# Fused attention plus mixture layer: score chunks of one key tile grouped before their exp drain

## The chip, the cores and the metric

One Trainium2 chip, all 8 NeuronCores, one launch. Times are device microseconds of the slowest core. The cores don't exchange data: each pair of cores takes one of four sequences. Even cores take query rows 0 to 2559 of it, odd cores rows 2560 to 4095.

## The reference, cut to what matters

The layer is feed-forward (8 experts, top 2), causal attention, feed-forward, each with a layer norm ahead and a residual. The change lies in the attention:

```python
q = jnp.concatenate([q_C.reshape(B, T, H, HS), q_R], axis=-1)
k = jnp.concatenate([k_C.reshape(B, T, H, HS), broadcast(k_R)], axis=-1)
att = jnp.einsum('bqhd,bkhd->bhqk', q, k) / jnp.sqrt(HS + DHR)
att = jnp.where(jnp.tril(jnp.ones((T, T), bool)), att, -jnp.inf)
att = softmax(att)
y = jnp.einsum('bhqk,bkhd->bqhd', att, v.reshape(B, T, H, HS)).reshape(B, T, C)
return y @ W_O
```

B = 4, T = 4096, C = 1024, H = 16, HS = 64, DHR = 32. Matmuls run in bf16 with fp32 accumulation.

## The kernel before, in words

Each engine (t PE, v DVE, s ACT, g POOL, y SP) gets a list of instructions that is written out by hand in the order of the Python code; an engine runs its list in order. `em.op` adds an instruction, `em.w` a wait on a semaphore, `em.drain` an instruction that ends when the engine's work ahead of it has ended and then signals. `Rot` hands out buffer slots in turn: `acquire` adds the waits that were left by whoever last released the slot.

The stages follow each other with a barrier between: layer norm, gate, feed-forward (first product at L381, second at L470), layer norm, keys and values, compressed queries (L698), then four quarters of four heads, each with a query stage (L756 and L759), a value stage and `attn_quarter`, and then the output projection, layer norm, gate and feed-forward. Even cores have 20 key tiles and 20 query tiles of 128 rows; odd cores have 32 key tiles and 12 query tiles (first query tile q0 = 20).

`attn_quarter` goes through its four heads. For each it builds the head's keys (L897), and then walks sections of up to 8 query tiles: an odd core has one section of 8 tiles and one of 4, an even core 8, 8 and 4. For each key tile of a section up to the last one its queries may see, the live queries are cut into chunks of up to 512. For one chunk PE writes scores to an accumulator slot (L927; three slots, PA0, PA1 and PM, rotation `pa_rot`), ACT takes the exponential into SBUF (L935; four buffers, `pt_rot`) and drains, on a key tile on the diagonal DVE multiplies the first 128 queries by the mask (L943), and PE multiplies by the values and adds into the section's accumulator `pav` of two banks (L960). Where a chunk crosses a bank, L960 is issued in two pieces. In PE's list the value matmul of a chunk stands right behind the wait for ACT's drain, and the next chunk's score matmul behind it. After a section, DVE takes a row of `pav`, SP moves it by a DMA, DVE takes the reciprocal (L980), PE spreads it over 64 rows (L992) and DVE scales (L996).

Of the kernel before, what the change touches and what calls it, by code (L numbers as in the profile page):

```python
# [864 lines left out]
def attn_quarter(em, d, s, p, nkt, ntt, q0, hq):  # L865
    S = em.sem
    pbig = p["big"]
    nk = nkt * 128

    secs = []  # L870
    t0 = 0
    while t0 < ntt:
        secs.append((t0, min(t0 + 8, ntt)))
        t0 += 8

    kh_rot = Rot(2, em)
    pa_rot = Rot(3)
    pt_rot = Rot(4)
    yev_rot = Rot(2, em)
    kc_rot = Rot(2)  # L880
    lsem = em.dsem()
    for hl in range(4):
        h = hq * 4 + hl
        ksl = kh_rot.acquire(em, "v")
        kh = s["khat"][:, ksl * T: ksl * T + T]
        em.op("v", lambda v, kh=kh: v.memset(kh[64:128, 0:nk], 0.0))
        em.drain("v", inc=S["DV"])
        dv_z = S["DV"].v
        em.w("y", S["DV"], dv_z)
        em.dma("y", kh[64:96, 0:nk], s["kr"][:, 0:nk], kh_rot.sems[ksl])  # L890
        em.dma("y", kh[96:97, 0:nk], d["onesr"][0:1, 0:nk], kh_rot.sems[ksl])
        la_kr = kh_rot.sems[ksl].v
        for tc in range(nk // 512):
            csl = kc_rot.acquire(em, "t")
            pk = pbig[0:64, PB1 + csl * 512: PB1 + csl * 512 + 512]
            for cc in range(2):
                em.op("t", lambda t, pk=pk, cc=cc, h=h, tc=tc: t.matmul(  # L897
                    pk, s["wukb"][:, cc * C + h * 64: cc * C + h * 64 + 64],
                    s["ckv"][:, cc * T + tc * 512: cc * T + tc * 512 + 512],
                    start=(cc == 0), stop=(cc == 1), skip_group_check=True),  # L900
                    inc=(S["PE"] if cc == 1 else None))
            pe_kc = S["PE"].v
            em.w("v", S["PE"], pe_kc)
            em.op("v", lambda v, kh=kh, pk=pk, tc=tc: v.tensor_copy(
                kh[0:64, tc * 512: tc * 512 + 512], pk), inc=S["DV"])
            kc_rot.release((S["DV"], S["DV"].v))
        em.drain("v", inc=S["DV"])
        dv_kh = S["DV"].v
        em.w("t", kh_rot.sems[ksl], la_kr)
        em.w("t", S["DV"], dv_kh)  # L910

        for (st_, en) in secs:
            seclen = (en - st_) * 128
            pav = pbig[0:65, PB0: PB0 + seclen]
            kmax = q0 + en
            first_kt = True
            for kt in range(kmax):
                qlo = max(st_, kt - q0)
                cols0 = qlo * 128
                ncols = (en - qlo) * 128  # L920
                diag = (kt - q0 == qlo and kt >= q0 + st_)
                for ch in range((ncols + 511) // 512):
                    cw = min(512, ncols - ch * 512)
                    co = cols0 + ch * 512
                    psl = pa_rot.acquire(em, "t")
                    ps = pbig[:, (PA0, PA1, PM)[psl]: (PA0, PA1, PM)[psl] + cw]
                    em.op("t", lambda t, ps=ps, kh=kh, kt=kt, hl=hl, co=co, cw=cw: t.matmul(  # L927
                        ps, kh[:, kt * 128:(kt + 1) * 128],
                        s["qh"][:, hl * NTMAX + co: hl * NTMAX + co + cw],
                        start=True, stop=True), inc=S["PE"])  # L930
                    pe_s = S["PE"].v
                    tsl = pt_rot.acquire(em, "s")
                    ptb = s["pt"][:, tsl * 512: tsl * 512 + cw]
                    em.w("s", S["PE"], pe_s)
                    em.op("s", lambda sc, ptb=ptb, ps=ps: sc.activation(  # L935
                        ptb, ps, AF.Exp), inc=S["AC"])
                    em.drain("s", inc=S["AC"])
                    ac_e = S["AC"].v
                    pa_rot.release((S["AC"], ac_e))
                    dv_m = None  # L940
                    if diag and ch == 0:
                        em.w("v", S["AC"], ac_e)
                        em.op("v", lambda v, ptb=ptb: v.tensor_mul(  # L943
                            ptb[:, 0:128], ptb[:, 0:128], s["dmask"][:, :]))
                        em.drain("v", inc=S["DV"])
                        dv_m = S["DV"].v
                    em.w("t", S["AC"], ac_e)
                    if dv_m is not None:
                        em.w("t", S["DV"], dv_m)
                    off0 = co - st_ * 128  # L950
                    pieces = []
                    o_, rel_ = off0, 0
                    while rel_ < cw:
                        w_ = min(cw - rel_, 512 - (o_ % 512))
                        pieces.append((o_, rel_, w_))
                        o_ += w_
                        rel_ += w_
                    for pi, (po, pr, pw) in enumerate(pieces):
                        em.op("t", lambda t, pav=pav, ptb=ptb, kt=kt, hl=hl,
                              po=po, pr=pr, pw=pw, fk=first_kt: t.matmul(  # L960
                            pav[:, po: po + pw],
                            s["vhat"][:, kt * 260 + hl * 65: kt * 260 + (hl + 1) * 65],
                            ptb[:, pr: pr + pw],
                            start=fk, stop=False, skip_group_check=True),
                            inc=(S["PE"] if pi == len(pieces) - 1 else None))
                    pt_rot.release((S["PE"], S["PE"].v))
                first_kt = False
            em.drain("t", inc=S["PE"])
            pe_av = S["PE"].v
            em.w("v", S["PE"], pe_av)  # L970
            em.op("v", lambda v, pav=pav, seclen=seclen: v.tensor_copy(
                s["lr"][64:65, 0:seclen], pav[64:65, 0:seclen]))
            em.drain("v", inc=S["DV"])
            dv_l = S["DV"].v
            em.w("y", S["DV"], dv_l)
            em.w("y", lsem, lsem.v)
            em.dma("y", s["lr"][0:1, 0:seclen], s["lr"][64:65, 0:seclen], lsem)
            la_l = lsem.v
            em.w("v", lsem, la_l)
            em.op("v", lambda v, seclen=seclen: v.reciprocal(  # L980
                s["lr"][0:1, 0:seclen], s["lr"][0:1, 0:seclen]))
            em.drain("v", inc=S["DV"])
            for ch in range((seclen + 511) // 512):
                cw = min(512, seclen - ch * 512)
                esl = yev_rot.acquire(em, "v")
                yb = s["yev"][0:64, esl * 512: esl * 512 + cw]
                em.op("v", lambda v, yb=yb, pav=pav, ch=ch, cw=cw: v.tensor_copy(
                    yb, pav[0:64, ch * 512: ch * 512 + cw]))
                em.drain("v", inc=S["DV"])
                em.w("t", S["DV"], S["DV"].v)  # L990
                prl = pbig[0:64, PM: PM + cw]
                em.op("t", lambda t, prl=prl, ch=ch, cw=cw: t.matmul(  # L992
                    prl, s["ones1f"][0:1, 0:64], s["lr"][0:1, ch * 512: ch * 512 + cw],
                    start=True, stop=True), inc=S["PE"])
                em.w("v", S["PE"], S["PE"].v)
                em.op("v", lambda v, yb=yb, prl=prl: v.tensor_tensor(  # L996
                    yb, yb, prl, ALU.mult))
                em.drain("v", inc=S["DV"])
                dv_y = S["DV"].v
                em.w("y", S["DV"], dv_y)  # L1000
                em.dma("y", d["d_yn"][h, :, q0 * 128 + st_ * 128 + ch * 512:
                                      q0 * 128 + st_ * 128 + ch * 512 + cw], yb,
                       yev_rot.sems[esl])
                yev_rot.release((yev_rot.sems[esl], yev_rot.sems[esl].v))
            em.w("t", S["DV"], S["DV"].v)
        kh_rot.release((S["PE"], S["PE"].v))
    yev_rot.finish(em, "y")
    kh_rot.finish(em, "y")
    em.w("y", lsem, lsem.v)
# [461 lines left out]
```

How the kernel before makes its waits and increments, by code:

```python
    def w(self, e, sem, val=None):  # L54
        if self.stopped:
            return
        v = sem.v if val is None else val
        if v <= 0:
            return
        self.q[e].append(lambda eng, s=sem.h, v=v: eng.wait_ge(s, v))
# [1 line left out]
    def op(self, e, fn, inc=None, n=1):  # L62
        if self.stopped:
            return None
        if inc is None:
            self.q[e].append(lambda eng, fn=fn: fn(eng))
            return None
        inc.v += n
        self.q[e].append(lambda eng, fn=fn, s=inc.h, n=n: fn(eng).then_inc(s, n))
        return inc.v
# [1 line left out]
    def drain(self, e, inc=None, n=1):  # L72
        if self.stopped:
            return None
        if inc is None:
            self.q[e].append(lambda eng: eng.drain())
            return None
        inc.v += n
        self.q[e].append(lambda eng, s=inc.h, n=n: eng.drain().then_inc(s, n))
        return inc.v
# [1 line left out]
    def dma(self, e, dst, src, sem):  # L82
        if self.stopped:
            return None
        sem.v += 16
        self.q[e].append(
            lambda eng, dst=dst, src=src, s=sem.h: eng.dma_start(dst, src).then_inc(s, 16))
        return sem.v
```

## Time and profile before

| | |
|---|---|
| median of 3 runs | 9474.25 us (9413.29 to 9484.06) |
| the profiled execution | 9392.34 us |
| its span, slowest core (7) | 9390.8 us |
| PE, DVE, ACT busy on that core | 5106.9, 1689.4, 1432.2 us |

The spans of odd cores are 9363 to 9391 us, those of even cores 9019 to 9031 us. The profile shows one core (the slowest, unless another is named). In the rows below a group or a timeline entry names line, engine, operation, output and input; "x" is a count; a number in square brackets is idle time of the engine just before, and what ended it. L79 is the helper that writes drains: "ACTq L79" is a drain on ACT's queue. "pbig" is the accumulator memory.

### The profile page before, as it was taken

How to read it: one execution, taken by the hardware profiler on the slowest of the kernel's cores; microseconds unless marked ns; L12 is line 12 of the kernel's file. 1: busy time of each engine (PE TensorE's matmuls, PEld its weight loads, DVE VectorE, ACT ScalarE, POOL GpSimd, SP SyncE). 2: the span in 40 equal slices, each digit the busy share in tenths (PEclk: the TensorE clock that was granted, in tenths of full speed). 3: DMA queues.
4: the chain of work that ended last, by engine and by line, in shares of the span. 5: the costliest groups of instructions: out<-in, count | busy, mean ns of one | idle time of the engine just before them, and what ended most of it. 6: DMA issues, size and time to landing. Idle time of an engine off the chain costs nothing.

```text
span 9390.8 us, 65490 instructions; the slowest of 8 cores (9019.2 to 9390.8 us)
## 1 busy us (share of the span) xinstructions
PE 5106.9 (54%) x18300; PEld 1838.5 (20%) x18300; DVE 1689.4 (18%) x3215; ACT 1432.2 (15%) x2340; POOL 302.3 (3%) x576
## 2 busy tenths in 40 slices
PE   1389996665565335534444444444444444359655
PEld 0234442222222112201101111101111111123222
DVE  4233330000000321121112111121112111223100
ACT  1033330000000100012220222022211222113000
POOL 0000000000000000100010000100010000010000
PEclk9999997777788668855556555655556555679877
DMA  4465543224333433300012000300011000466343
GB/s 163 115 160 156 158 149 63 61 61 96 98 92 101 159 110 91 91 7 3 2 15 60 2 2 3 71 2 2 4 27 46 2 2 3 139 156 165 74 103 94
DMA packets 874165, 683.01 MB, mean 73 GB/s; under 512 B 489584, under 2 KB 791664, under 8 KB 873152
## 3 DMA queue, kind: packets, MB, share of 16 engines
q1 hardware_dynamic: 792224, 584.56, 21.9%
q0 software_dynamic: 81584, 94.16, 6.1%
q8 instruction: 167, 2.74, 0.1%
q14 instruction: 190, 1.56, 0.1%
HBM read 582.45 MB, written 180.36 MB: 81 GB/s over the span
## 4 chain that ended last, share of the span: by engine, by line
PE 46%; DMA 16%; DVE 9%; ACT 9%; SPq 6%; issue 6%; DVEq 2%; POOL 2%; PEldq 1%; ACTq 1%; PEld 0%; POOLq 0%
PE pbig L470 15%; PE pbig L381 12%; PE pbig L960 8%; ACT sb_pt L935 8%; SPq L87 6%; PE pbig L927 6%; DMA sb_hld<-d_h 5%; DMA sb_xnld<-d_xnA 2%; DVEq L79 2%; DMA sb_cqld<-d_cq 2%; DMA d_cq<-sb_cqst 2%; DVE sb_lr L980 2%; PE pbig L756 1%; DMA sb_xt<-d_x 1%; PE pbig L992 1%
## 5 line engine op out<-in xcount | busy, mean ns | idle before, releaser
L470 PE MATMUL pbig<-sb_w2b,sb_hld 128*128 128x512 bf16 x5632 | 1402.9, 414 | 978.0 <-DMA sb_hld<-d_h 978.0
L960 PE MATMUL pbig<-sb_pt,sb_vhat 128*65 128x512 bf16 (+3 forms) x1392 | 782.1, 569 | 1220.4 <-ACTq L79 1003.2
L381 PE MATMUL pbig<-sb_xnld,sb_w1b 128*128 128x512 bf16 x5632 | 1264.1, 386 | 123.0 <-DMA sb_xnld<-d_xnA 123.0
L935 ACT ACTIVATE sb_pt<-pbig 128x512 bf16<-128x512 f32 (+1 forms) x1344 | 771.8, 574 | 2309.5 <-PE pbig L927 2309.5
L470 PEld LDWEIGHTS pbig<-sb_w2b,sb_hld 128*128 128x128 bf16 x5632 | 581.4, 105 | 1779.3 <-issue 1241.7
L927 PE MATMUL pbig<-sb_qh,sb_khat 128*128 128x512 bf16 (+1 forms) x1344 | 809.1, 602 | 34.8 <-DVEq L79 34.8
L381 PEld LDWEIGHTS pbig<-sb_xnld,sb_w1b 128*128 128x128 bf16 x5632 | 551.9, 99 | 813.4 <-issue 190.0
L393 ACT ACTIVATE sb_hrelu<-pbig,sb_b1c 128x512 bf16<-128x512 f32 x704 | 483.9, 687 | 1394.5 <-PE pbig L381 1337.8
L402 DVE TENSOR_TENSOR sb_hst<-sb_hrelu,pbig 128x512 bf16<-128x512 bf16 x704 | 473.9, 686 | 978.6 <-ACT sb_hrelu L393 568.1
L960 PEld LDWEIGHTS pbig<-sb_pt,sb_vhat 128*65 128x65 bf16 x1392 | 179.4, 132 | 2217.8 <-issue 2217.8
L943 DVE TENSOR_TENSOR sb_pt<-sb_pt,sb_dmask 128x128 bf16<-128x128 bf16 x192 | 43.2, 225 | 2495.4 <-ACTq L79 2495.4
L756 PE MATMUL pbig<-sb_cqld,sb_wuqh 128*128 128x512 bf16 x768 | 249.4, 408 | 280.7 <-DMA sb_wqrh<-wqr 161.0
L192 ACT ACTIVATE sb_sqs<-sb_xt 128x1024 bf16<-128x1024 f32 x76 | 80.3, 1056 | 1910.6 <-DMA sb_xt<-d_x 1889.3
L246 PE MATMUL pbf<-sb_cidb,sb_xnt 128*128 128x128 bf16 x608 | 76.9, 306 | 502.1 <-DVEq L79 502.1
L698 PE MATMUL pbig<-sb_xnld,sb_wdqh 128*128 128x512 bf16 x768 | 194.7, 403 | 135.7 <-DVE sb_cqst L706 71.8
L992 PE MATMUL pbig<-sb_lr,sb_ones1f 1*64 1x512 f32 x96 | 92.8, 1068 | 317.8 <-DVEq L79 317.8
L503 DVE TENSOR_TENSOR sb_ypld<-sb_ypld,pbig 128x1024 f32<-128x1024 f32 x44 | 53.7, 1221 | 1172.1 <-PE pbig L480 1122.6
L491 DVE COPY sb_yt<-pbig 128x1024 f32<-128x1024 f32 x44 | 53.9, 1225 | 1069.8 <-PE pbig L470 1069.8
L87 POOL DMA_DIRECT2D sb_wuqh<-wuq x128 | 102.8, 803 | 3187.4 <-SPq L79 3187.4
L811 ACT ACTIVATE sb_q2s<-sb_qh 96x512 bf16<-96x512 bf16 x48 | 30.2, 630 | 1097.3 <-DVEq L79 964.1
L980 DVE RECIPROCAL sb_lr<-sb_lr 1x1024 f32<-1x1024 f32 (+1 forms) x32 | 158.1, 4941 | 61.0 <-DMA sb_lr<-sb_lr 61.0
L246 PEld LDWEIGHTS pbf<-sb_cidb,sb_xnt 128*128 128x128 bf16 x608 | 58.8, 137 | 520.1 <-issue 520.1
(112 smaller groups left out, 2351.5 us busy)
## 6 DMA issues: line engine op xcount, KB each, us to landing
sb_xnld<-d_xnA SPq DMA_DIRECT2D x704, 128.0 KB, 2.9
d_h<-sb_hst SPq DMA_DIRECT2D x704, 128.0 KB, 1.9
sb_hld<-d_h SPq DMA_DIRECT2D x352, 256.0 KB, 4.7
sb_xt<-d_x SPq DMA_DIRECT2D x112, 512.0 KB, 5.0
sb_xt<-x SPq DMA_DIRECT2D x96, 512.0 KB, 5.3
sb_cqld<-d_cq SPq DMA_DIRECT2D x384, 128.0 KB, 2.2
sb_w1b<-w POOLq DMA_DIRECT2D x128, 256.0 KB, 9.1
sb_w2b<-w POOLq DMA_DIRECT2D x128, 256.0 KB, 20.6
```

What stands on the lines that cost most here:

```text
L79: self.q[e].append(lambda eng, s=inc.h, n=n: eng.drain().then_inc(s, n))
L87: lambda eng, dst=dst, src=src, s=sem.h: eng.dma_start(dst, src).then_inc(s, 16))
L381: em.op("t", lambda t, ph=ph, wsl=wsl, xsl=xsl, xc=xc, ht=ht: t.matmul(ph, s["w1b"][:, wsl * 8 * C + xc * C + ht * 128: wsl * 8 * C + xc * ...
L393: em.op("s", lambda sc, rb=rb, ph=ph, e=e, ht=ht: sc.activation(rb, ph, AF.Relu, bias=s["b1c"][:, e * 8 + ht: e * 8 + ht + 1]), inc=S["AC"])
L402: em.op("v", lambda v, ob=ob, rb=rb, pw=pw: v.tensor_tensor(ob, rb, pw, ALU.mult), inc=S["DV"])
L470: half=half, k=k, last=last, pa=pa: t.matmul(ph, s["hld"][:, lsl * 4096 + ei * 1024 + hc * 128: lsl * 4096 + ei * 1024 + hc * 128 + 128], ...
L698: em.op("t", lambda t, ps=ps, xsl=xsl, xc=xc, cq=cq: t.matmul(ps, s["wdqh"][:, xc * 2048 + cq * 128: xc * 2048 + cq * 128 + 128], s["xnld" ...
L756: em.op("t", lambda t, ps=slots[dt], cqc=cqc, dt=dt, cl=cl: t.matmul(ps, s["wuqh"][:, cqc * 256 + dt * 128: cqc * 256 + dt * 128 + 128], c ...
L927: em.op("t", lambda t, ps=ps, kh=kh, kt=kt, hl=hl, co=co, cw=cw: t.matmul(ps, kh[:, kt * 128:(kt + 1) * 128], s["qh"][:, hl * NTMAX + co: ...
L935: em.op("s", lambda sc, ptb=ptb, ps=ps: sc.activation(ptb, ps, AF.Exp), inc=S["AC"])
L960: po=po, pr=pr, pw=pw, fk=first_kt: t.matmul(pav[:, po: po + pw], s["vhat"][:, kt * 260 + hl * 65: kt * 260 + (hl + 1) * 65], ptb[:, pr: p ...
L980: em.op("v", lambda v, seclen=seclen: v.reciprocal(s["lr"][0:1, 0:seclen], s["lr"][0:1, 0:seclen]))
```

## The change

All chunks of a key tile (two where more than 512 queries are live, else one) now form a group. First come the score matmul and the exp of every chunk, each with its own slots, without a drain between the exps; then one drain of ACT, whose value releases all score slots of the group; the mask multiply of a diagonal tile and PE wait for that one value; then come all value matmuls.

```diff
+                chinfo = []
                 for ch in range((ncols + 511) // 512):
...
                     em.op("s", lambda sc, ptb=ptb, ps=ps: sc.activation(
                         ptb, ps, AF.Exp), inc=S["AC"])
-                    em.drain("s", inc=S["AC"])
-                    ac_e = S["AC"].v
-                    pa_rot.release((S["AC"], ac_e))
-                    dv_m = None
-                    if diag and ch == 0:
-                        em.w("v", S["AC"], ac_e)
-                        em.op("v", lambda v, ptb=ptb: v.tensor_mul(
-                            ptb[:, 0:128], ptb[:, 0:128], s["dmask"][:, :]))
-                        em.drain("v", inc=S["DV"])
-                        dv_m = S["DV"].v
-                    em.w("t", S["AC"], ac_e)
-                    if dv_m is not None:
-                        em.w("t", S["DV"], dv_m)
+                    chinfo.append((psl, tsl, ptb, co, cw))
+                em.drain("s", inc=S["AC"])
+                ac_grp = S["AC"].v
+                for psl, _, _, _, _ in chinfo:
+                    pa_rot.release_slot(psl, (S["AC"], ac_grp))
+                dv_m = None
+                if diag:
+                    em.w("v", S["AC"], ac_grp)
+                    em.op("v", lambda v, ptb=chinfo[0][2]: v.tensor_mul(
+                        ptb[:, 0:128], ptb[:, 0:128], s["dmask"][:, :]))
+                    em.drain("v", inc=S["DV"])
+                    dv_m = S["DV"].v
+                em.w("t", S["AC"], ac_grp)
+                if dv_m is not None:
+                    em.w("t", S["DV"], dv_m)
+                for psl, tsl, ptb, co, cw in chinfo:
                     off0 = co - st_ * 128
                     pieces = []
...
-                    pt_rot.release((S["PE"], S["PE"].v))
+                    pt_rot.release_slot(tsl, (S["PE"], S["PE"].v))
```

PE's list on an odd core, first key tiles of the section of 8 query tiles, with each instruction's waits (AC is ACT's semaphore, DV is DVE's, D9 a DMA's), before:

```order
L927 MATMUL pbig<-sb_qh,sb_khat 128x512 [waits D9,DV]
L960 MATMUL pbig<-sb_pt,sb_vhat 65x512 [waits AC]
L927 MATMUL pbig<-sb_qh,sb_khat 128x512
L960 MATMUL pbig<-sb_pt,sb_vhat 65x512 [waits AC]
L927 MATMUL pbig<-sb_qh,sb_khat 128x512
```

and of the changed kernel (scores are L928 there, values L964):

```order
L928 MATMUL pbig<-sb_qh,sb_khat 128x512 [waits D9,DV]
L928 MATMUL pbig<-sb_qh,sb_khat 128x512
L964 MATMUL pbig<-sb_pt,sb_vhat 65x512 [waits AC]
L964 MATMUL pbig<-sb_pt,sb_vhat 65x512
L928 MATMUL pbig<-sb_qh,sb_khat 128x512
```

The second score matmul of a key tile moved ahead of the first value matmul, and one of two waits on ACT before a value matmul is gone.

The same list at key tile 21, with 512 and 384 live queries, on the diagonal, before:

```order
L927 MATMUL pbig<-sb_qh,sb_khat 128x512 [waits AC]
L960 MATMUL pbig<-sb_pt,sb_vhat 65x384 [waits AC,DV]
L960 MATMUL pbig<-sb_pt,sb_vhat 65x128
L927 MATMUL pbig<-sb_qh,sb_khat 128x384 [waits AC]
L960 MATMUL pbig<-sb_pt,sb_vhat 65x384 [waits AC]
L927 MATMUL pbig<-sb_qh,sb_khat 128x512 [waits AC]
```

and of the changed kernel:

```order
L928 MATMUL pbig<-sb_qh,sb_khat 128x512 [waits AC]
L928 MATMUL pbig<-sb_qh,sb_khat 128x384 [waits AC]
L964 MATMUL pbig<-sb_pt,sb_vhat 65x384 [waits AC,DV]
L964 MATMUL pbig<-sb_pt,sb_vhat 65x128
L964 MATMUL pbig<-sb_pt,sb_vhat 65x384
L928 MATMUL pbig<-sb_qh,sb_khat 128x512 [waits AC]
```

The wait for the mask (DV) now stands behind both score matmuls; the pieces of the value matmul are the same. The order of ACT's exps and of DVE's instructions is unchanged.

## Rows read from the trace of the kernel before

**Rows 1.** Spans and granted clock of an even and an odd core
```profile
core 6: 9026.7 us, clock 0.710
...
core 7: 9390.8 us, clock 0.705
```

**Rows 2.** The page's chain that ended last, shares by line
```profile
PE pbig L470 15%; PE pbig L381 12%; PE pbig L960 8%; ACT sb_pt L935 8%; SPq L87 6%; PE pbig L927 6%; DMA sb_hld<-d_h 5%; DMA sb_xnld<-d_xnA 2%; DVEq L79 2%; DMA sb_cqld<-d_cq 2%; DMA d_cq<-sb_cqst 2%; DVE sb_lr L980 2%; PE pbig L756 1%; DMA sb_xt<-d_x 1%; PE pbig L992 1%
```

**Rows 3.** Source line L935 (ns min/median/max, starts), and L927's 512-column group by form
```profile
L935 ACT ACTIVATE sb_pt<-pbig x1344: 277/597/598, 4118.7 to 8023.1; 128x512 bf16<-128x512 f32 x176, 128x384 bf16<-128x384 f32 x16
...
L927 PE MATMUL pbig<-sb_qh,sb_khat 128*128 128x512 bf16 x1200 | 748.7, 624 | 34.8 <-DVEq L79 34.8
```

**Rows 4.** Core 7, timeline in a section of 8 query tiles (start us, us)
```profile
7900.36 0.61 PE L960 MATMUL pbig<-sb_pt,sb_vhat 128*65 128x512 bf16 x1 [0.87 <-ACTq L79]
...
7900.76 0.63 PE L927 MATMUL pbig<-sb_qh,sb_khat 128*128 128x512 bf16 x1
7901.49 0.60 ACT L935 ACTIVATE sb_pt<-pbig 128x512 bf16<-128x512 f32 x1 [1.31 <-PE pbig L927]
...
7902.26 0.61 PE L960 MATMUL pbig<-sb_pt,sb_vhat 128*65 128x512 bf16 x1 [0.87 <-ACTq L79]
...
7913.70 0.61 PE L960 MATMUL pbig<-sb_pt,sb_vhat 128*65 128x512 bf16 x1 [0.87 <-ACTq L79]
```

**Rows 5.** Timeline of PE alone, matmuls back to back in L756
```profile
3893.83 1.01 PE L756 MATMUL pbig<-sb_cqld,sb_wuqh 128*128 128x512 bf16 x2 [42.05 <-DMA sb_wqrh<-wqr]
...
3895.06 1.06 PE L756 MATMUL pbig<-sb_cqld,sb_wuqh 128*128 128x512 bf16 x2
3895.91 0.63 PE L759 MATMUL pbig<-sb_cqld,sb_wqrh 128*128 128x512 bf16 x1
```

**Rows 6.** Timeline: ACT at L192, and the first exp of a quarter
```profile
3176.51 1.06 ACT L192 ACTIVATE sb_sqs<-sb_xt 128x1024 bf16<-128x1024 f32 x1
3177.48 0.18 ACT L192 ACTIVATION_READ_ACCUMULATOR sb_sqs<-sb_xt 128x1 f32 x1
...
4116.97 0.38 PE L927 MATMUL pbig<-sb_qh,sb_khat 128*128 128x512 bf16 x1 [0.98 <-DVEq L79]
4117.43 1.28 ACT L935 ACT_TABLE_LOAD   x1 [51.69 <-PE pbig L927]
4118.72 0.60 ACT L935 ACTIVATE sb_pt<-pbig 128x512 bf16<-128x512 f32 x1
```

**Rows 7.** Timeline of L927 on key tiles 21, 22 and 23 of that section
```profile
4200.71 0.52 PE L927 MATMUL pbig<-sb_qh,sb_khat 128*128 128x384 bf16 x1
...
4202.30 0.63 PE L927 MATMUL pbig<-sb_qh,sb_khat 128*128 128x512 bf16 x1
...
4204.56 0.42 PE L927 MATMUL pbig<-sb_qh,sb_khat 128*128 128x256 bf16 x1
...
4205.83 0.63 PE L927 MATMUL pbig<-sb_qh,sb_khat 128*128 128x512 bf16 x1
...
4208.09 0.31 PE L927 MATMUL pbig<-sb_qh,sb_khat 128*128 128x128 bf16 x1
...
4209.18 0.59 PE L927 MATMUL pbig<-sb_qh,sb_khat 128*128 128x512 bf16 x1
```

**Rows 8.** Busy us in four stretches, then granted clock, DMA share, GB/s
```profile
core 7: us, PE busy (x) PEld busy (x) DVE busy (x) ACT busy (x) POOL busy (x), PEclk, DMA share, GB/s
2160.00:2168.00 8.00, 4.99 (x12) 1.75 (x13) 0.00 (x0) 0.00 (x0) 0.00 (x0) 0.50 0.25 48
...
3892.00:3900.00 8.00, 6.17 (x16) 2.31 (x17) 0.00 (x0) 0.00 (x0) 0.00 (x0) 0.53 0.28 62
3900.00:3904.00 4.00, 3.79 (x17) 1.19 (x15) 0.00 (x0) 0.00 (x0) 0.00 (x0) 1.00 0.56 161
4117.00:4217.00 100.00, 51.12 (x107) 12.03 (x107) 1.80 (x8) 31.06 (x53) 0.00 (x0) 0.51 0.00 0
```

**Rows 9.** The page's row of the other activation that reads the accumulator
```profile
L393 ACT ACTIVATE sb_hrelu<-pbig,sb_b1c 128x512 bf16<-128x512 f32 x704 | 483.9, 687 | 1394.5 <-PE pbig L381 1337.8
```

## The prediction

> **What bounds the kernel now.** I read the spans of the cores first: an odd core takes 9390.8 us and an even one 9026.7 us [rows 1], so the odd cores (32 key tiles, 12 query tiles) set the time. The profiled execution was measured at 9392.34 us, 1.5 us more than that span. The page's chain [rows 2] is spread over stages, and its lines L960, L935 and L927, all of the attention's inner loop, have about equal shares: 8%, 8% and 6%. Three engines taking turns on one chain look like that. On an odd core exps run from 4118.7 to 8023.1 us [rows 3].
>
> The timeline of that loop shows the turns [rows 4]. Per chunk of 512 queries: the score matmul L927 starts, the exp L935 starts 0.73 us later, the value matmul L960 starts 0.77 us after the exp's start (0.60 of exp, 0.17 for its drain and the signal to PE), and the next score matmul starts 0.40 us after that. The period is 1.906 us ((7913.70 - 7900.36) / 7). PE idles 0.87 us in each, waiting for ACT's drain; ACT idles 1.31, waiting for PE. No two chunks overlap. All score chunks of 512 on this core number 1200 [rows 3]. So in this stage latency in series bounds, not an engine.
>
> **The change, part by part.** Only key tiles whose live queries exceed 512 have two chunks. Of an odd core's head, the section of 8 query tiles walks key tiles 0 to 27: 21 (0 to 20) have 512+512, tiles 21, 22, 23 have 512+384, 512+256, 512+128, and the last four one chunk. The section of 4 query tiles walks 32 key tiles with one chunk each. That is 24 pairs and 36 single chunks, 84 chunks a head, 1344 for 16 heads, the count of L935 [rows 3]. For a single chunk nothing moves in the order. So 384 pairs change: 336 full ones and 16 of each shorter kind.
>
> Before, a full pair costs 2 x 1.906 = 3.81 us [rows 4]. After, PE issues S0 S1, ACT E0 E1 and one drain, PE AV0 AV1, then the next S0:
> - S0 to E0: 0.73 us, as before. S1 starts 0.43 us after S0 (two matmuls at 1.2 GHz start 0.85 us before the third [rows 5]) and is ready at 0.43 + 0.73 = 1.16 us.
> - E0 to E1. No row has an exp right behind an exp. Bounds: an ACT instruction behind an ACTIVATE starts 0.97 us after one of 1.06 us, so 0.09 us early; the exp behind the table load starts 0.01 us after its end (4118.72 against 4117.43 + 1.28) [rows 6]. So 0.51 or 0.61 us. I take 0.51, since that row has an ACTIVATE ahead with no drain between, as here. E1 then starts at 1.24 us, 0.08 us after S1 is ready: the second score matmul hides behind the first exp, but hardly more than that.
> - E1 to AV0: 0.77 us, with the drain that was there before. AV0 no longer starts after E0 alone; that costs nothing of its own, since before, PE had only S1 to run behind it.
> - AV0 to AV1 0.40 us, AV1 to the next S0 0.43 us.
>
> Sum 0.73 + 0.51 + 0.77 + 0.40 + 0.43 = 2.84 us; a full pair saves 0.97 us. What goes is one S-to-exp latency (0.73) and one drain with its signal (0.17), and 0.09 of exp overlap; about 0.02 is lost in spacing.
>
> The ScalarE page of the Trainium skill (ScalarE: Activation LUTs, section What ACT_TABLE_LOAD costs) says that back-to-back ACTIVATEs overlap by about 93 ns. No row here shows it for two exps. By that rule E0 to E1 is about 0.50 us and the sum stays as it is; by the table-load row it would be 327 us instead of 365.
>
> The shorter pairs: the second chunk costs 1.59 us now with 384 queries (4200.71 to 4202.30), 1.27 with 256, 1.09 with 128 [rows 7]. After, it adds its exp less the 0.09 us of overlap, and its value matmul. The exp is 0.28 us at 128 columns and 0.60 at 512 [rows 3], so 0.107 per 128 more; the matmul is 0.43 us at 512 in proportion. That is 0.40 + 0.32, 0.29 + 0.21 and 0.19 + 0.11 us: it saves 0.87, 0.77 and 0.79 us.
>
> The mask multiply on DVE stands after the exp and ahead of the value matmul before and after, once per diagonal tile; it now starts after both exps, and that wait is already counted. Queued behind PE's one wait for the group are AV0, AV1 and the next S0, which waited for the same chain before. The score buffers: three slots, two to a group; the slots that a group takes were freed by the drain of the group before it or of an earlier one, and PE has waited for that drain already, ahead of AV0. The exp buffers: four slots, each free two groups later. Both at nothing. An odd core loses one ACT drain per pair, 384 of 1344. No DMA, and nothing of POOL or SP, moves.
>
> Sum for an odd core: per head 21 x 0.97 + 0.87 + 0.77 + 0.79 = 22.8 us; x 16 = 365 us. 9392 - 365 = 9027 us against the profiled execution. An even core has 10 full and 6 shorter pairs a head: about 14.6 x 16 = 233 us, so 9027 - 233 = 8794, and the odd cores still end last. The profiled execution lies under the three timed runs (9413, 9474, 9484); the mean of the four is 9441 us, and I subtract from that: 9076, say 9080 us. With runs 1% apart like this, about 1% is what a measurement of this kernel can tell from no change.
>
> **Rivals.**
> - *The exps don't overlap* (0.61 between them). For it: the table-load row [rows 6], and that E1 waits for its own matmul's signal. Against: the accumulator row. A full pair saves 0.87, the sum is 365 - 384 x 0.10 = 327 us: 9114 us.
> - *Something later gives part back.* Cores run their last stages a few per cent otherwise aligned, and L470, 15% of the chain [rows 2], and its loads from memory may wait more. For it: the even cores move 130 us less than the odd ones. Against: the stage itself moves almost nothing by DMA (0.00 share in a section) [rows 8]. Price 20 to 60 us: 9100 to 9140.
> - *The clock rises.* In a section PE is at the 1.2 GHz level (granted 0.51) with PE busy 51 of 100 us [rows 8]. In the new pair it is busy about 0.40 + 0.43 + 0.43 + 0.63 = 1.89 of 2.84 us, 67%. If that lifted it to 2.4 GHz, the three spacings of 0.40 to 0.43 would be about half, and S0 to E0 about 0.48 (the first score matmul, at that level, took 0.38 in place of 0.63 [rows 6]): 0.48 + 0.51 + 0.77 + 0.22 + 0.22 = 2.20, another 0.64 x 336 = 215 us: 8865 us. Against: eight microseconds with 4.99 us of matmuls, 62%, stayed at 0.50; the level rose after 3892:3900, where PE ran without a gap once it had started at 3893.83 [rows 5, 8]. The new loop keeps an ACT gap of about 0.95 us in every 2.84.
> The TensorE page of the Trainium skill (TensorE: Matmul & The Clock Gate, section A second HAM failure mode: psum-queue depth-cycling) describes kernels with short idles between matmul groups that swing between both levels. By that part of the pairs would run at the faster one; the 62% row speaks against it.
> - *No gain*: S1 is held back until AV0, so that the change does not do what it says. Against: the order puts both score matmuls ahead, and their slot waits are on drains already passed. It gives 9441 us.
> - *Slower*: now the first exp reads the accumulator while PE writes the next chunk's scores. Before they never met. If that slowed both, say each exp to twice its 0.60 and S1 held to E0's end, a pair would be 2.84 + 1.20 + 0.43 = 4.47 us, 0.66 over today: 9441 + 253 = 9694 us. It decides from 0.97 us of extra a pair. Against: L393 reads the accumulator under a continuous stream of L381 matmuls in 687 ns mean, with a bias operand, against 0.60 us here [rows 9]. That leaves a tenth of what it needs.
>
> **How the numbers follow.** The forecast 0.64; exps without overlap 0.14; part given back 0.11; clock 0.06; no gain 0.03; slower 0.02. The range takes in the first three: low 8970 (the profiled execution less 365 is 9027, with some pairs at the higher clock), high 9170 (9484 - 327 is 9157). It leaves out most of the clock case, and no gain and slower, and some scatter. Faster by over 1%: 0.95; within 1%: 0.03; slower: 0.02.
>
> **What would show it.** In the changed profile's timeline of a section of 8 query tiles: two score matmuls 0.43 us apart, two exps 0.51 apart, period 2.84 us; if 2.94, the exps don't overlap. That section (100 us in rows 8) should take about 77 us, the one of 4 tiles the same as before. PE waits for ACT's drain once a group, 60 times a head in place of 84. Granted clock about 0.51 there. Other stages unchanged. I am wrong if the period in a pair is above 3.1 us or below 2.6, or if sections with single chunks change.

## The result, and the profile after

The changed kernel took 9104.73 us (median of 10 runs, 9025.63 to 9164.39); the kernel before, over its own 10 runs, 9458.69 us (9387.43 to 9512.00). The ratio is 0.962, with a 95% interval of 0.958 to 0.966: 3.8% faster. The profiled execution was measured at 9112.65 us. I had forecast 9080 us, and 365 us off a mean of 9441, which is a ratio of 0.961.

The spans and granted clocks of the changed kernel:

```profile
core 0: 8792.6 us, clock 0.717
core 1: 9019.9 us, clock 0.712
...
core 6: 8883.3 us, clock 0.707
core 7: 9111.1 us, clock 0.704
```

Core 1 went from 9389.6 us to 9019.9 us, 370 less. Core 7, the slowest, became only 280 us shorter than its span before [rows 1]. The difference does not come from the changed code: on core 7 the attention begins 106 us later than on core 1, after a feed-forward stage (L381) that was not touched. The busy times in that stage, for two odd cores of one die:

```profile
core 5: us, PE busy (x) PEld busy (x) DVE busy (x) ACT busy (x) POOL busy (x), PEclk, DMA share, GB/s
500.00:1000.00 500.00, 457.02 (x2045) 199.03 (x2043) 169.14 (x252) 173.08 (x252) 25.37 (x48) 0.96 0.58 157
...
core 7: us, PE busy (x) PEld busy (x) DVE busy (x) ACT busy (x) POOL busy (x), PEclk, DMA share, GB/s
500.00:1000.00 500.00, 473.34 (x1787) 190.67 (x1784) 150.31 (x220) 151.14 (x220) 21.13 (x40) 0.80 0.51 138
```

The granted clock (the number after the busy times) is 0.96 on core 5 and 0.80 on core 7, and core 7 got 1787 matmuls into the 500 us where core 5 did 2043. Below, the times of the attention itself are therefore read off its own rows, and not off a span. The page's head and chain, to set beside [rows 2]:

```profile
span 9111.1 us, 64722 instructions; the slowest of 8 cores (8792.6 to 9111.1 us)
...
PE 47%; DMA 17%; DVE 10%; SPq 7%; issue 6%; ACT 5%; ACTq 4%; DVEq 2%; POOL 2%; PEldq 1%; PEld 0%; POOLq 0%
PE pbig L470 15%; PE pbig L381 13%; PE pbig L964 8%; SPq L87 7%; PE pbig L928 6%; DMA sb_hld<-d_h 5%; ACT sb_pt L936 4%; ACTq L79 3%; DVEq L79 2%; DMA d_cq<-sb_cqst 2%; DVE sb_lr L984 2%; DMA sb_xnld<-d_xnA 2%; DMA sb_cqld<-d_cq 2%; PE pbig L756 2%; DMA sb_xt<-d_x 1%
```

The exps' share fell from 8% to 4% (L936 is what L935 was; L928 is L927, L964 is L960), and the matmuls kept theirs. The pair itself, in a section of 8 query tiles, as the timeline has it (start us, length us), beside the single turns of [rows 4]:

```profile
7610.18 1.03 PE L964 MATMUL pbig<-sb_pt,sb_vhat 128*65 128x512 bf16 x2 [0.93 <-ACTq L79]
...
7611.01 1.06 PE L928 MATMUL pbig<-sb_qh,sb_khat 128*128 128x512 bf16 x2
...
7611.74 1.09 ACT L936 ACTIVATE sb_pt<-pbig 128x512 bf16<-128x512 f32 x2 [1.73 <-PE pbig L928]
...
7613.00 1.03 PE L964 MATMUL pbig<-sb_pt,sb_vhat 128*65 128x512 bf16 x2 [0.93 <-ACTq L79]
```

The merged rows show two score matmuls (1.06 us from the first start to the second end), then two exps in 1.09 us, then two value matmuls. From one pair of value matmuls to the next it is 2.82 us. Scores to exps 0.73, exps to values 1.26, values to the next scores 0.83.

The whole section of 8 query tiles, and behind it the one of 4:

```profile
core 7: us, PE busy (x) PEld busy (x) DVE busy (x) ACT busy (x) POOL busy (x), PEclk, DMA share, GB/s
4219.00:4296.00 77.00, 46.63 (x107) 12.87 (x107) 1.97 (x9) 28.45 (x53) 0.00 (x0) 0.51 0.00 0
4313.00:4375.00 62.00, 31.95 (x64) 7.40 (x64) 1.76 (x6) 18.47 (x32) 0.00 (x0) 0.50 0.01 1
```

The first held 107 matmuls in 77 us where [rows 8] has the same 107 in 100 us. The clock did not move (0.51 and 0.51), and ACT's busy time fell from 31.06 to 28.45 us only because two exps now overlap. The second section has 64 matmuls in 62 us; in the trace its first and last matmul lie 60.7 us apart, as before. Who waits, for the exps' line and then the values':

```profile
L936 ACT ACTIVATE sb_pt<-pbig x1344: 272/597/598, 4221.1 to 7752.4; 128x512 bf16<-128x512 f32 x176, 128x384 bf16<-128x384 f32 x16
...
  PE pbig L928: 2185.0, 960
```

```profile
L964 PE MATMUL pbig<-sb_pt,sb_vhat x1392: 284/607/634, 4222.4 to 7753.2; 128*65 128x512 bf16 x164, 128*65 128x384 bf16 x13, 128*65 128x256 bf16 x12, 128*65 128x128 bf16 x10
...
  ACTq L79: 703.2, 768
  DVEq L79: 220.2, 192
```

PE waited 768 times for ACT's drain and 192 times for the mask: 960 groups, 60 a head, in place of 84 chunks.

### The profile page after: what moved, and what is told of

It is laid out like the page before. It is cut to its first block, busy times and chain, and to the rows that moved or that the text cites. A ratio compares the mean times of both kernels' runs of the same rounds, so it can differ in the third digit from the quotient of the medians.

```text
span 9111.1 us, 64722 instructions; the slowest of 8 cores (8792.6 to 9111.1 us)
## 1 busy us (share of the span) xinstructions
PE 5138.3 (56%) x18300; PEld 1871.0 (21%) x18300; DVE 1694.5 (19%) x3215; ACT 1390.8 (15%) x2340; POOL 302.3 (3%) x576
## 4 chain that ended last, share of the span: by engine, by line
PE 47%; DMA 17%; DVE 10%; SPq 7%; issue 6%; ACT 5%; ACTq 4%; DVEq 2%; POOL 2%; PEldq 1%; PEld 0%; POOLq 0%
PE pbig L470 15%; PE pbig L381 13%; PE pbig L964 8%; SPq L87 7%; PE pbig L928 6%; DMA sb_hld<-d_h 5%; ACT sb_pt L936 4%; ACTq L79 3%; DVEq L79 2%; DMA d_cq<-sb_cqst 2%; DVE sb_lr L984 2%; DMA sb_xnld<-d_xnA 2%; DMA sb_cqld<-d_cq 2%; PE pbig L756 2%; DMA sb_xt<-d_x 1%
## 5 line engine op out<-in xcount | busy, mean ns | idle before, releaser
L470 PE MATMUL pbig<-sb_w2b,sb_hld 128*128 128x512 bf16 x5632 | 1402.5, 414 | 987.6 <-DMA sb_hld<-d_h 987.6
L381 PE MATMUL pbig<-sb_xnld,sb_w1b 128*128 128x512 bf16 x5632 | 1381.1, 412 | 92.8 <-DMA sb_xnld<-d_xnA 91.6
L964 PE MATMUL pbig<-sb_pt,sb_vhat 128*65 128x512 bf16 (+3 forms) x1392 | 710.7, 574 | 923.4 <-ACTq L79 703.2
L936 ACT ACTIVATE sb_pt<-pbig 128x512 bf16<-128x512 f32 (+1 forms) x1344 | 730.3, 573 | 1978.5 <-PE pbig L928 1978.2
L470 PEld LDWEIGHTS pbig<-sb_w2b,sb_hld 128*128 128x128 bf16 x5632 | 580.2, 105 | 1789.8 <-issue 1251.3
L381 PEld LDWEIGHTS pbig<-sb_xnld,sb_w1b 128*128 128x128 bf16 x5632 | 578.4, 104 | 871.6 <-issue 547.3
L928 PE MATMUL pbig<-sb_qh,sb_khat 128*128 128x512 bf16 (+1 forms) x1344 | 727.9, 599 | 34.3 <-DVEq L79 34.3
L964 PEld LDWEIGHTS pbig<-sb_pt,sb_vhat 128*65 128x65 bf16 x1392 | 154.4, 139 | 1661.0 <-issue 1658.2
L756 PE MATMUL pbig<-sb_cqld,sb_wuqh 128*128 128x512 bf16 x768 | 245.6, 403 | 281.1 <-DMA sb_wqrh<-wqr 161.8
L192 ACT ACTIVATE sb_sqs<-sb_xt 128x1024 bf16<-128x1024 f32 x76 | 80.3, 1056 | 1918.7 <-DMA sb_xt<-d_x 1899.3
L698 PE MATMUL pbig<-sb_xnld,sb_wdqh 128*128 128x512 bf16 x768 | 191.1, 397 | 137.8 <-DVE sb_cqst L706 74.8
L928 PEld LDWEIGHTS pbig<-sb_qh,sb_khat 128*128 128x128 bf16 x1344 | 171.1, 127 | 254.3 <-issue 244.6
L811 ACT ACTIVATE sb_q2s<-sb_qh 96x512 bf16<-96x512 bf16 x48 | 30.2, 630 | 1092.9 <-DVEq L79 957.6
```

What stands on the lines that cost most here:

```text
L381: em.op("t", lambda t, ph=ph, wsl=wsl, xsl=xsl, xc=xc, ht=ht: t.matmul(ph, s["w1b"][:, wsl * 8 * C + xc * C + ht * 128: wsl * 8 * C + xc * ...
L470: half=half, k=k, last=last, pa=pa: t.matmul(ph, s["hld"][:, lsl * 4096 + ei * 1024 + hc * 128: lsl * 4096 + ei * 1024 + hc * 128 + 128], ...
L698: em.op("t", lambda t, ps=ps, xsl=xsl, xc=xc, cq=cq: t.matmul(ps, s["wdqh"][:, xc * 2048 + cq * 128: xc * 2048 + cq * 128 + 128], s["xnld" ...
L756: em.op("t", lambda t, ps=slots[dt], cqc=cqc, dt=dt, cl=cl: t.matmul(ps, s["wuqh"][:, cqc * 256 + dt * 128: cqc * 256 + dt * 128 + 128], c ...
L936: em.op("s", lambda sc, ptb=ptb, ps=ps: sc.activation(ptb, ps, AF.Exp), inc=S["AC"])
L964: po=po, pr=pr, pw=pw, fk=first_kt: t.matmul(pav[:, po: po + pw], s["vhat"][:, kt * 260 + hl * 65: kt * 260 + (hl + 1) * 65], ptb[:, pr: p ...
```

## The experiments

Eight kernels ran. In each the section of 8 query tiles of core 7 (52 score matmuls, 52 value matmuls and 3 more pieces at bank borders: 107) is the yardstick: it lasts from its first score matmul to its last value matmul, and is 99.5 us before and 76.3 us after for the first head of a quarter, 97.7 and 74.5 for a later one.

### e1: the overlap without the saved drain

```diff
                     em.op("s", lambda sc, ptb=ptb, ps=ps: sc.activation(
                         ptb, ps, AF.Exp), inc=S["AC"])
+                    em.drain("s", inc=S["AC"])
                     chinfo.append((psl, tsl, ptb, co, cw))
-                em.drain("s", inc=S["AC"])
                 ac_grp = S["AC"].v
```

> The changed kernel, but ACT drains after each exp of a pair; both score matmuls still go first and the value matmuls still wait for the last drain. My theory: the change gains by hiding the second score matmul behind the first exp, and a second, small part comes from the drain that is gone. So the second exp should start 0.68 us after the first (0.60 and about 0.08 for the drain) in place of 0.49, the pair should take 3.01 us in place of 2.82, and a section of 8 query tiles about 79 us in place of 74.5 to 76.3: still about 290 us below the kernel before. Rival, the gain is the drain's: a pair should be back near 3.81 us and the section near 98 us.

It took 9203.38 us (one run; before on the same chip 9447.55, median of 7). The timeline of one pair:

```profile
4139.88 1.03 PE L964 MATMUL pbig<-sb_pt,sb_vhat 128*65 128x512 bf16 x2 [1.27 <-ACTq L79]
...
4141.43 0.60 ACT L936 ACTIVATE sb_pt<-pbig 128x512 bf16<-128x512 f32 x1 [1.74 <-PE pbig L928]
4142.25 0.60 ACT L936 ACTIVATE sb_pt<-pbig 128x512 bf16<-128x512 f32 x1 [0.22 <-issue]
...
4143.03 1.03 PE L964 MATMUL pbig<-sb_pt,sb_vhat 128*65 128x512 bf16 x2 [1.27 <-ACTq L79]
```

The pair is 3.15 us and the section 84.2 us, where I expected 3.01 and 79. My number for the second exp was too low: it starts 0.82 us after the first, not 0.68, since a drain leaves ACT idle for 0.22 us. The direction held: all of the sections together, 2544.2 us on core 7 before, are 2304.5 us here and 2172.3 us in the changed kernel. So 240 of the 372 us come without any drain being saved. The rival, that it is all the drain's, is out; but the drain's part, 132 us or 0.34 us a pair, is more than my 0.17 + 0.09.

### e3: one drain, without the overlap

```diff
                     psl = pa_rot.acquire(em, "t")
+                    if ch == 1:
+                        em.w("t", S["AC"], S["AC"].v)
                     ps = pbig[:, (PA0, PA1, PM)[psl]: (PA0, PA1, PM)[psl] + cw]
```

> The changed kernel, but PE holds the second score matmul of a pair back until the first exp has signalled its end; one drain a pair and the joint wait stay. My theory: with the overlap gone the pair is 0.73 + 0.60 + 0.10 (signal) + 0.73 + 0.77 + 0.83 = 3.76 us, a section about 97 us, within 30 us of the kernel before. Rival, the gain comes from the single drain and joint wait: the pair stays under 3.4 us and the section under 88 us.

It took 9416.16 us (one run). The timeline:

```profile
4201.48 1.03 PE L966 MATMUL pbig<-sb_pt,sb_vhat 128*65 128x512 bf16 x2 [0.87 <-ACTq L79]
...
4202.31 0.63 PE L930 MATMUL pbig<-sb_qh,sb_khat 128*128 128x512 bf16 x1
4203.03 0.60 ACT L938 ACTIVATE sb_pt<-pbig 128x512 bf16<-128x512 f32 x1 [1.74 <-PE pbig L930]
...
4203.78 0.59 PE L930 MATMUL pbig<-sb_qh,sb_khat 128*128 128x512 bf16 x1 [0.84 <-ACT sb_pt L938]
4204.46 0.60 ACT L938 ACTIVATE sb_pt<-pbig 128x512 bf16<-128x512 f32 x1 [0.83 <-PE pbig L930]
...
4205.23 1.03 PE L966 MATMUL pbig<-sb_pt,sb_vhat 128*65 128x512 bf16 x2 [0.87 <-ACTq L79]
```

The second score matmul starts 0.75 us after the first exp's start, the pair takes 3.75 us as expected, and the sections sum to 2526.6 us. The single drain and the joint wait alone give 18 us of the 372. The three numbers don't add: overlap alone 240, single drain alone 18, both 372. My reading is that the drain between the exps costs ACT time that only shows once the second chunk's scores are ready and ACT is what the pair waits for.

### e2: each value matmul waits for its own exp

```diff
-                em.w("t", S["AC"], ac_grp)
-                if dv_m is not None:
-                    em.w("t", S["DV"], dv_m)
-                for psl, tsl, ptb, co, cw in chinfo:
+                for ci, (psl, tsl, ptb, co, cw, ac_e) in enumerate(chinfo):
+                    em.w("t", S["AC"], ac_e)
+                    if dv_m is not None and ci == 0:
+                        em.w("t", S["DV"], dv_m)
```

(and a drain behind each exp, as in e1).

> Both score matmuls of a pair first, a drain after each exp, and each value matmul waits for its own exp alone, so that the first can run beside the second exp. My theory (latency in series sets the pace): the pair is 0.73 + 0.68 + 0.77 + 0.43 = 2.61 us, 0.21 less than in the changed kernel, section about 70 us, and 0.21 x 384 = 80 us less in all, about 9020 us, ratio to before 0.953. Rival, the group wait costs nothing because PE or ACT is full: no change against the changed kernel, or 0.19 us more a pair for the second drain (ratio 0.970).

It took 9030.10 us (median of 4); the ratio to before is 0.958, interval 0.951 to 0.966, which does not part it from the changed kernel. The trace does:

```profile
4141.42 1.06 PE L928 MATMUL pbig<-sb_qh,sb_khat 128*128 128x512 bf16 x2
...
4142.15 0.60 ACT L936 ACTIVATE sb_pt<-pbig 128x512 bf16<-128x512 f32 x1 [1.31 <-PE pbig L928]
...
4142.93 0.61 PE L963 MATMUL pbig<-sb_pt,sb_vhat 128*65 128x512 bf16 x1 [0.45 <-ACTq L79]
4142.97 0.60 ACT L936 ACTIVATE sb_pt<-pbig 128x512 bf16<-128x512 f32 x1 [0.22 <-issue]
...
4143.75 0.61 PE L963 MATMUL pbig<-sb_pt,sb_vhat 128*65 128x512 bf16 x1 [0.21 <-ACTq L79]
...
4144.15 1.06 PE L928 MATMUL pbig<-sb_qh,sb_khat 128*128 128x512 bf16 x2
```

The first value matmul (4142.93) starts 0.04 us ahead of the second exp (4142.97) and is hidden by it. The pair is 2.73 us, 0.12 above my number by the drain's 0.14 again, and the sections sum to 2126.6 us, 46 less than the changed kernel's 2172.3. The joint wait thus cost one value matmul a pair, 0.42 us of 3.15 (e1 against e2), and the change paid for it with the drain it saved.

### e7: pairs everywhere

```diff
-            for kt in range(kmax):
...
+            for g0 in range(0, len(chunks), 2):
+                grp = []
+                for kt, co, cw, dg in chunks[g0:g0 + 2]:
```

Chunks are paired in their order, over key tiles too; the form of a pair is the change's.

> The change's own form (two score matmuls, two exps, one drain, two value matmuls) for every two chunks in a row, over key tiles too, so that the section of 4 query tiles and the last key tiles are paired as well. My theory: each pair saves 0.99 us wherever it stands, so the section of 4 tiles goes from 60.7 to about 46 us, and an odd core saves 16 x 17 = 270 us more than the changed kernel, about 8800 us, ratio 0.932. Rival, the saving hangs on both chunks using the same keys or on a full section of two banks: the section stays over 55 us, ratio over 0.95.

It took 8814.18 us (median of 2), ratio 0.933, interval 0.922 to 0.944. The section of 4 query tiles:

```profile
4271.00:4317.00 46.00, 29.09 (x64) 7.70 (x64) 1.48 (x6) 16.73 (x32) 0.00 (x0) 0.50 0.01 2
```

64 matmuls in 46 us (44.8 us from first to last, 60.7 before), and all sections together 1884.3 us, 288 less than the changed kernel. I had expected 270. The saving belongs to any two chunks in flight, not to two chunks of one key tile: the rival is out.

### e4: one chunk ahead all the time

```diff
+            for n in range(min(LOOK, len(chunks))):
+                score(n)
+            for n in range(len(chunks)):
+                if n + LOOK < len(chunks):
+                    score(n + LOOK)
```

Here `score(n)` emits a chunk's score matmul, exp and drain, and the value matmul of chunk n follows with a wait for its own exp; LOOK is 1.

> The kernel before, but PE issues the score matmul of the next chunk ahead of the value matmul of this one throughout a section, across key tiles; one drain per exp, the same buffers. My theory: two chunks in flight share the latency, (0.40 + 0.73 + 0.77) / 2 = 0.95 us a chunk at the 1.2 GHz level, and since PE then runs almost without a gap the clock rises and it is (0.22 + 0.48 + 0.77) / 2 = 0.73 us. An odd core saves (1.906 - 0.73) x 1344 = 1580 us, an even one 1.17 x 960 = 1125 us, so that the even cores end last, at about 7900 us, ratio 0.837 (0.866 if the clock stays low). Rival, the accumulator or ACT limits once they overlap (each exp stretched when PE writes beside it): over 1.2 us a chunk and exps over 0.70 us, ratio above 0.90.

It took 8158.86 us (median of 4), ratio 0.864, interval 0.859 to 0.869. Two turns of it, and the section:

```profile
4150.68 0.38 PE L977 MATMUL pbig<-sb_pt,sb_vhat 128*65 128x512 bf16 x1 [0.23 <-ACTq L79]
4150.72 0.60 ACT L943 ACTIVATE sb_pt<-pbig 128x512 bf16<-128x512 f32 x1 [0.22 <-PE pbig L935]
...
4150.89 0.38 PE L935 MATMUL pbig<-sb_qh,sb_khat 128*128 128x512 bf16 x1
...
4151.49 0.38 PE L977 MATMUL pbig<-sb_pt,sb_vhat 128*65 128x512 bf16 x1 [0.23 <-ACTq L79]
4151.54 0.60 ACT L943 ACTIVATE sb_pt<-pbig 128x512 bf16<-128x512 f32 x1 [0.22 <-PE pbig L935]
```

```profile
core 7: us, PE busy (x) PEld busy (x) DVE busy (x) ACT busy (x) POOL busy (x), PEclk, DMA share, GB/s
4126.00:4173.00 47.00, 31.62 (x107) 10.92 (x107) 2.00 (x9) 31.05 (x53) 0.00 (x0) 0.91 0.00 1
```

The section of 52 chunks takes 46.5 us, and its granted clock is 0.91 where [rows 8] has 0.51: PE's matmuls last 0.38 us (the 2.4 GHz level) in place of 0.61 and 0.63. A turn is 0.82 us, not my 0.73: the exps are 0.82 us apart, so ACT with its drain seems to set the pace, and PE waits 0.23 us each time. The total missed my 7900 us, since core 0's sections fell by 891 us (1805.3 to 914.6) and not by 1125: with its many masked and short chunks one took 0.95 us on average there. The rival of stretched exps is out: they last 0.60 us as before. The even cores end last (8153.0 us against 8029.4 for core 7), as expected. How much of the gain the clock gives was not parted from the rest; without its rise I had expected 0.95 us a chunk.

### e5: two chunks ahead

```diff
-LOOK = 1
+LOOK = 2
```

> As e4 (score matmuls run ahead over key tiles), but two chunks ahead in place of one, still a drain after each exp. e4 took 0.82 us a chunk, the distance of two exps with a drain between (0.60 and 0.22), so my theory now is that ACT with its drains sets the pace there and not the latency: no gain from the second chunk ahead, 0.82 us a chunk, sections of 44 and 27 us on an odd core. Rival, the latency still decides in e4: a third less, about 0.6 us a chunk and sections under 36 us.

It took 8070.16 us (median of 2, 8032.06 and 8108.27). The exps in the timeline of ACT:

```profile
4190.31 0.60 ACT L943 ACTIVATE sb_pt<-pbig 128x512 bf16<-128x512 f32 x1 [0.22 <-PE pbig L935]
4191.13 0.60 ACT L943 ACTIVATE sb_pt<-pbig 128x512 bf16<-128x512 f32 x1 [0.22 <-PE pbig L935]
```

Again 0.82 us apart; the section is 43.6 us (42.4 for a later head) against 46.5 (44.5). What is left of the second chunk ahead is the start of a section and the tiles with a mask: in the first 6 us of the section and on its masked tiles e4's exps start up to 1.4 us apart, and e5's nowhere more than 0.82. So in between ACT and its drain bound e4; the rival that the latency still decides is out.

### e6: three ahead, no drain behind an exp

```diff
-LOOK = 1
-SLOTS = (PA0, PA1, PM)
+LOOK = 3
+SLOTS = (PA0, PA1, PM, PB1)
...
-                em.drain("s", inc=S["AC"])
                 ac_e = S["AC"].v
                 pa_rot.release_slot(psl, (S["AC"], ac_e))
+                ac_e += 1
+                if n == len(chunks) - 1:
+                    em.drain("s", inc=S["AC"])
```

> Three chunks ahead, four score slots (the fourth in accumulator columns 2048 to 2559, free there), and no drain after an exp: the value matmul and the mask wait for the end of the exp behind the one they need, and the section's last exp is drained. My theory: ACT sets the pace at the 0.49 us of two exps with nothing between (as in the changed kernel), PE needs 0.43 at 2.4 GHz: 0.50 us a chunk, sections of about 28 and 18 us on an odd core, even cores last at about 7750 us, ratio 0.82. Rival, the drain was not what held ACT (the accumulator or the clock is): 0.8 us a chunk as in e4, ratio 0.864.

It took 7954.75 us (median of 6), ratio 0.841, interval 0.833 to 0.849: 16% under the kernel before. ACT's timeline in a section of 4 query tiles, and the section of 8:

```profile
4258.10 13.09 ACT L943 ACTIVATE sb_pt<-pbig 128x512 bf16<-128x512 f32 x27 [0.18 <-PE pbig L935]
```

```profile
4206.00:4237.00 31.00, 26.79 (x107) 11.10 (x107) 1.93 (x10) 26.59 (x53) 0.00 (x0) 0.94 0.00 1
```

27 exps in 13.09 us without a gap are 0.48 us each. Sections take 30.2 and 18.3 us (27.4 and 18.2 for the next head), as expected; all of core 7's together 763.1 us of the 2544.2 before. This run changes three things against e4 (chunks ahead, a fourth score slot, no drains), and its gain is that of all three. The total missed my 0.82. On even core 2 the sections fell from 1806.7 us (read on core 6, also even, since core 2's trace before lacks some matmul records) to 620.6, 1186 less, but its span only from 9030.9 to 7940.9, 1090 less. In the last feed-forward stage core 2 looks so:

```profile
core 2: us, PE busy (x) PEld busy (x) DVE busy (x) ACT busy (x) POOL busy (x), PEclk, DMA share, GB/s
6200.00:6700.00 500.00, 465.50 (x1800) 192.02 (x1835) 153.30 (x226) 154.72 (x227) 33.83 (x64) 0.84 0.58 153
```

The clock is granted at 0.84, and the stage's first half, from the first L381 matmul to the first L470, lasts 718 us where it lasted 648 before. It is tempting to blame core 3, which shares core 2's sequence and now reaches the same stage sooner. But core 3's last L381 begins at 6538 us, and in the trace's record of the clock core 2 stands at 0.81, with short drops, from 6165 to 6412 us already. On core 0 the same half, also beside an odd core's, lasts 652 us. The last section comes back to this.

### e8: two ahead, no drain

```diff
-LOOK = 3
-SLOTS = (PA0, PA1, PM, PB1)
+LOOK = 2
+SLOTS = (PA0, PA1, PM)
```

> e6 with two chunks ahead and the three score slots of before, no drain after an exp. My theory: a score matmul goes out only 0.22 us after the value matmul two chunks before it, and its value matmul must also wait for the next exp, so latency decides again: (0.22 + 0.48 + 0.60 + 0.10) / 2 = 0.70 us a chunk, sections of about 38 and 23 us. Rival, ACT decides here too: 0.50 us a chunk as in e6.

It took 8127.90 us (one run). The timeline of ACT's rows:

```profile
4285.23 1.09 ACT L943 ACTIVATE sb_pt<-pbig 128x512 bf16<-128x512 f32 x2 [0.43 <-PE pbig L935]
...
4286.66 1.09 ACT L943 ACTIVATE sb_pt<-pbig 128x512 bf16<-128x512 f32 x2 [0.34 <-PE pbig L935]
```

Two exps together every 1.43 us (4285.23 to 4286.66) are 0.72 us a chunk, and ACT idles 0.34 us between. The sections take 40.9 and 25.1 us (39.4 and 25.4 for the next head), against an expected 38 and 23. With no drain, two chunks ahead and three slots are too few: latency sets the pace again, and the rival that ACT does is out. All sections of core 7 sum to 1042.4 us, 78 less than e5's 1120.7. The time does not follow, and the even cores end last: core 6, the slowest here, has sections of 818.7 us in all against 806.7 in e5. The first section of each head, where all eight key tiles carry a mask, grew (162.6 to 187.6 us for all heads), the other two shrank (369.7 to 366.2 and 274.3 to 264.9).

## Why the prediction was right

*The bound.* Three engines in turn, no engine full: right. e4 and e6 took 54% and 70% of the attention's sections away on core 7 (1170.5 and 763.1 us of 2544.2) with the same matmuls and exps.

*The pair.* Each term of the sum, forecast and measured: S0 to E0 0.73 and 0.73; E0 to AV0 0.51 + 0.77 = 1.28 and 1.26; from the first value matmul to the next score matmul 0.83 and 0.83 (7610.18 to 7611.01); sum 2.84 and 2.82. Two exps take 1.09 us, so they overlap by 0.60 + 0.60 - 1.09 = 0.11, where I took 0.09 from the accumulator row. Unrounded, exps of 597 ns start 493 ns apart, 104 ns of overlap. The rule of the Trainium skill (ScalarE: Activation LUTs, section What ACT_TABLE_LOAD costs) gives 93 ns for it, and the trace agrees to about 0.01 us. The rival without overlap falls, and so does that of no gain: the second score matmul is not held back. The shorter pairs, read on key tiles 21 to 23, save 0.89, 0.78 and 0.81 us, forecast 0.87, 0.77 and 0.79.

*Which sections move.* The section of 8 query tiles fell by 23.2 us (99.5 to 76.3, and 97.7 to 74.5), forecast 22.8; the one of 4 did not move. All sections of core 7: 2544.2 - 2172.3 = 372 us, forecast 365. Core 1's span fell by 370, the median of the runs by 354. The even cores ended first, as forecast: core 0 fell from 9019.2 to 8792.6 us, 227 less against 233.

*Where the saving comes from.* This step was loosely put. I split it into the hidden scores (0.73), the drain (0.17) and the overlap of exps (0.09). The sum was right, the shares were not: hiding the scores behind an exp and its drain gives 3.81 - 3.15 = 0.66, and dropping the drain then gives 0.33, since between two exps a drain leaves ACT idle for 0.22 us and also keeps them from overlapping. I read the 0.17 off the row from the exp's end to the value matmul, which is another path: from ACT to PE.

*The clock.* It stayed at 0.51 with two chunks in flight, as forecast, though PE's busy share in the section rose from 51 to 61% (46.63 of 77 us), and in a full pair to the 67% that I had worked out (idle 0.93 of 2.82 us). It rose to 0.91 in e4, where PE's gaps are 0.23 us. So the rival's mechanism is real, but two chunks with a gap of 0.93 us behind them don't set it off. The Trainium skill (TensorE: Matmul & The Clock Gate, section A second HAM failure mode: psum-queue depth-cycling) speaks of a swing between the levels; the pair shows none.

*Something given back later.* Not in the changed kernel: the spans of cores 1 and 0 fell by 370 and 227 us, and their sections had given 374 and 232. Core 7 lost about 100 us ahead of the attention, in code that did not change.

*Slower, because ACT reads the accumulator beside PE's writes.* Exps last 597 ns in the median and 598 at most in the changed kernel, as before; in e6, with PE hardly ever idle, their median is 603 ns on core 7 and 619 ns on core 1, and the longest 633 and 636. If that is the effect, it is 1 to 4%, far from the doubling that the rival needs.

## What to carry to other kernels

Where a timeline shows engines taking turns, add the distances start to start round the loop; what a second independent piece in flight saves can then be summed beforehand (2.84 us against 2.82 measured). Grouping is the first step of that, and running ahead without groups is worth much more: 3.8% for pairs in a key tile and 6.7% for pairs everywhere against 13.6% with one chunk ahead and 15.9% with three ahead, a fourth slot and no drains between exps. What a drain costs is read between two instructions of its own engine (0.82 against 0.49 us here), not on the way to the engine that waits.

## What was not expected of the hardware

A drain between two exps costs 0.33 us, over half an exp: 0.22 of idle and 0.11 of lost overlap (e1, against the changed kernel).

The granted clock has a value between 1.2 and 2.4 GHz in dense stages. Two odd cores of one die in the changed kernel's profile:

```profile
core 5: us, PE busy (x) PEld busy (x) DVE busy (x) ACT busy (x) POOL busy (x), PEclk, DMA share, GB/s
900.00:1000.00 100.00, 95.80 (x431) 41.85 (x430) 35.36 (x53) 36.37 (x53) 4.24 (x8) 0.98 0.56 160
...
900.00:1000.00 100.00, 100.00 (x379) 40.30 (x377) 32.23 (x47) 31.69 (x47) 0.00 (x0) 0.81 0.40 123
```

